# A GRU's state update on VectorE in another order, and the reset product's passes in another order on TensorE

## The chip, the core and the metric

One NeuronCore of a Trainium2 chip runs the whole kernel. The metric is the device time of one execution in microseconds (us); less is better.

## The reference

x is [32, 512, 512] (batch, time, features), the state has 512 features. A conditioned GRU runs over the 512 time steps, and its states are added to x:

```python
vz = video @ C_z + b_z          # vr, vh alike
xz = einsum('btd,de->bte', seq, W_z)   # xr, xh alike
def step(h, xs):
    z = sigmoid(xz_t + h @ U_z + vz)
    r = sigmoid(xr_t + h @ U_r + vr)
    hh = tanh(xh_t + (r * h) @ U + vh)
    h_new = (1 - z) * h + z * hh
```

Everything is float32. Each step needs the state of the one before.

## The kernel before

**Layout.** The 32 x 512 state lies on 128 partitions as four groups of 32 rows, with 128 columns each: partition group j holds features 128 j to 128 j + 127. A 32 x 32 block transpose on VectorE ("turn") makes of it the weights of the next product. Each product is cut into 4 x 4 matmuls of 32 weight columns: q counts the part that is summed over, j the partition group that is written.

**Precision.** x, the gates' weights and the state are split into a high and a low part in float16 (h_hi and h_lo for the state; ur_hi and ur_lo, uz_hi and uz_lo for the weights). Three passes of products, high x high, high x low and low x high, stand for one in float32. The candidate product alone runs in float32.

**One time step,** by the engines' own queues; semaphores alone order them against each other:
- TensorE (`step`, L356 on): the reset product (`reset_product`, L296, its matmul L303, 48 matmuls of 128 columns), the update product (L312, 48), three groups of the x projection of two steps ahead (L276, 12 matmuls of 384 columns), the candidate product (L266, two halves, each after its reset_t), in every fourth step a small total product (L285), and the other nine groups of the projection (36 matmuls). Then the next step's reset product.
- ScalarE: h_hi of half 0 and half 1 from the turned state (L428), the reset gate in two halves (L432), 1 - z and z (L435, L436), the candidate's tanh in two halves (L441), and in three steps of four one operation on x for a later set of steps (L382, L385 or L388).
- VectorE (`go_on` and `begin`): the reset state r * h and its turn for each half (L637, L639), the seeds of the next accumulators with the projections (L518, L523), a turn of x (L514), then for each half `take` (L661: tanh times z), `renew` (L665: plus the kept part, which gives the new state) and `turn` (L669: into h_t), and h_lo for each half (L611: h_t times 2 to the 14th minus h_hi).
- GpSimd: the kept part (1 - z) * h (L223), the low part of x (L210), and x plus the new state (L237), which is sent out by SyncE's queue in blocks of 8 steps.

The halves are halves of the 128 columns, so two of the four q of the next product each: reset_product waits for h_hi of half 0, h_lo of half 0, h_hi of half 1, h_lo of half 1, each ahead of the first pass that uses it. The order on each engine is written out by hand; nothing plans it. The loop on TensorE holds 4 steps, those of the others 64. TensorE's last pass through `step` stands for no time step: the engines raise its semaphores by hand.

Of the kernel before, what the change touches and what calls it, by code (L numbers as in the profile page):

```python
# [5 lines left out]
def conditioned_gru_residual_kernel(nc, x, cond, W_z, U_z, C_z, b_z, W_r, U_r, C_r, b_r, W_h, U_h, C_h, b_h, out):  # L6
# [24 lines left out]
    HALVES = 2  # L31
# [22 lines left out]
    with ctx:  # L54
# [70 lines left out]
        def half(a):  # L125
            return slice(N // HALVES * a, N // HALVES * (a + 1))
# [10 lines left out]
        def part(j):  # L137
            return slice(B * j, B * (j + 1))

        def cols(c):  # L140
            return slice(N * c, N * (c + 1))
# [107 lines left out]
        def _(pe):  # L249
# [44 lines left out]
                total(p_bank[k][:, G * N + c:G * N + c + 1], row_sum, [x_sum[:, of:of + 1]], first).then_inc(x_totaled, 1)  # L294

            def reset_product(out, halves):  # L296
                passes = [(h, a, b) for h in range(HALVES) for a in range(2) for b in range(2 - a)]
                for n, (h, a, b) in enumerate(passes):
                    if b == 0:
                        pe.wait_ge((h_hi_ready, h_lo_ready)[a], halves[h])  # L300
                    for q in range(Q // HALVES * h, Q // HALVES * (h + 1)):
                        for j in range(J):
                            last = nc.tensor.matmul(out[part(j)], (h_hi, h_lo)[a][:, part(q)], ur[b][:, q, cols(j)],  # L303
                                                    start=False, stop=n == len(passes) - 1 and q == Q - 1,
                                                    skip_group_check=True)
                return last
# [49 lines left out]
            def step(m, tt):  # L356
                s = m * SET + tt
                c, k = tt % SET, tt % 2
                now = pe.snap(s + 1)
                halves = [pe.snap(HALVES * s + (a + 1)) for a in range(HALVES)]  # L360
                pe.wait_ge(seeded, now)
                reset_product(cell(k, R), halves).then_inc(r_mm, 1)
                update_product(cell(k, Z)).then_inc(z_mm, 1)
                pe.wait_ge(c_seeded, now)
                pe.wait_ge(x_t_ready, pe.snap(s + 3))
                project(k, (c + 2) % SET, 0, BEFORE_C)
                candidate_product([(reset_t_ready, a) for a in halves])
                if c == TOTAL_STEP:
                    total_x(TOTAL_STEP % 2, 0, 0, pe.snap(m + (tt // SET + 3)), False)
                project(k, (c + 2) % SET, BEFORE_C, GROUPS)  # L370
# [110 lines left out]
        def _(dve):  # L481
# [19 lines left out]
            def least_x(k, m, count):  # L501
                dve.wait_ge(x_link, count(2 * m + 1))
                V.tensor_scalar(x_pow[k][:], x_pow[k][:], LEAST, None, ALU.max).then_inc(x_link, 1)

            def up_x(k, m, count):
                dve.wait_ge(x_link, count(2 * m + 2))
                up_of(x_up[k][:], x_pow[k][:]).then_inc(x_scaled, 1)
# [4 lines left out]
            def turn_x(k, c, sets):  # L512
                dve.wait_ge(x_lo_ready, sets)
                V.transpose(x_t[:, c].rearrange("p n a -> p (n a)").bitcast(i32),  # L514
                            x_parts[k][:, cols(c)].rearrange("p n a -> p (n a)").bitcast(i32)).then_inc(x_t_ready, 1)

            def seed_gates(k, d):
                V.scalar_tensor_tensor(banks[k][:, :, 0:N], p_bank[k][:, 0:GATES * N].rearrange("p (g n) -> p g n", g=GATES),  # L518
                                       x_down[d][:, W_GATES:W_GATES + 1], base[:, 0:GATES], ALU.mult, ALU.add)\
                    .then_inc(seeded, 1)  # L520
# [99 lines left out]
            def go_on(i, tt, last):  # L620
                s = i * STEPS + tt
                m, t = divmod(tt, SET)
                now_m = i * (STEPS // SET) + m
                old, new = state[:, (tt - 1) % SLOTS], state[:, tt % SLOTS]

                def count(v):
                    return v if last else dve.snap(v)

                now = count(s + 1)

                def more(sets):
                    return not (last and m + sets >= STEPS // SET)

                for a in range(HALVES):
                    ready = count(HALVES * s + (a + 1))
                    dve.wait_ge(r_gate, ready)
                    V.tensor_tensor(reset[:, half(a)], gate_r[:, half(a)], old[:, half(a)], ALU.mult).then_inc(reset_ready, 1)  # L637
                    dve.wait_ge(reset_ready, ready)
                    V.transpose(reset_t[:, half(a)], reset[:, half(a)]).then_inc(reset_t_ready, 1)  # L639

                if t == POWER_STEP and more(2):
                    least_x(m % 2, now_m + 2, count)
                if not (last and tt == STEPS - 1):
                    if t == SET - 1:
                        dve.wait_ge(x_down_ready, count(now_m + 2))
                    dve.wait_ge(projected, count(s + 2))
                    seed_gates((tt + 1) % 2, (tt + 1) // SET % 2)
                if t == POWER_STEP and more(2):
                    up_x(m % 2, now_m + 2, count)
                dve.wait_ge(kept_ready, now)  # L650
                if last and tt >= STEPS - TURN_AHEAD:
                    dve.sem_inc(x_t_ready, 1)
                else:
                    ahead_m, c = divmod(tt + TURN_AHEAD, SET)
                    turn_x(ahead_m % 2, c, count(s + (TURN_AHEAD + 1)))

                ready = [count(HALVES * s + (a + 1)) for a in range(HALVES)]

                def take(a):
                    dve.wait_ge(c_gate, ready[a])  # L660
                    V.tensor_tensor(taken[:, half(a)], gate_c[:, half(a)], gate_z[:, half(a)], ALU.mult).then_inc(taken_ready, 1)  # L661

                def renew(a):
                    dve.wait_ge(taken_ready, ready[a])
                    V.tensor_tensor(new[:, half(a)], taken[:, half(a)], kept[:, half(a)], ALU.add).then_inc(h_ready, 1)  # L665

                def turn(a):
                    dve.wait_ge(h_ready, ready[a])
                    V.transpose(h_t[:, half(a)], new[:, half(a)]).then_inc(h_t_ready, 1)  # L669

                take(0)
                renew(0)
                take(1)
                turn(0)
                if last and tt == STEPS - 1:
                    dve.sem_inc(seeded, 1)
                    dve.sem_inc(c_seeded, 1)
                    dve.sem_inc(h_lo_ready, HALVES)
                    dve.sem_inc(reset_t_ready, HALVES)
                renew(1)  # L680
                turn(1)

            begin(0, 0, True)
# [1 line left out]
            with nc.Fori(0, PASSES - 1, engines=[dve.engine], hint_back_edge=True, head_slot={dve.engine: DVE_SLOT}) as i:  # L685
                for tt in range(STEPS):
                    go_on(i, tt, False)
                    begin(i, tt + 1, False)
            for tt in range(STEPS):
                go_on(PASSES - 1, tt, True)  # L690
                if tt < STEPS - 1:
                    begin(PASSES - 1, tt + 1, True)
# [24 lines left out]
```

## Time and profile before

| | us |
|---|---|
| median of 3 runs | 2236.66 (2235.65 to 2237.01) |
| the profiled execution itself | 2234.19 |
| its span, first to last instruction | 2232.4 |
| TensorE matmuls busy | 2179.1 (98%) |
| VectorE busy | 1751.8 (78%) |
| ScalarE busy | 1326.2 (59%) |
| GpSimd busy | 689.1 (31%) |
| granted TensorE clock, mean | 0.999 of full speed |

In the views PE is TensorE's matmuls, PEld its weight loads (which run beside matmuls), DVE VectorE, ACT ScalarE, POOL GpSimd. L303 is line 303 of the kernel. An engine starts an operation before the recorded end of the one ahead of it where nothing holds it, so spacings are read from start to start. The records of matmuls overlap in the same way: four of them, one for each j, run side by side. Rows are rounded to 0.01 us.

### The profile page before, as it was taken

What the parts mean: (1) busy time and instruction counts of PE and PEld (TensorE: products, weight loads), DVE (VectorE), ACT (ScalarE), POOL (GpSimd) and SP (SyncE); (2) the same over time, 40 slices, a digit from 0 to 9 for tenths busy, and PEclk for the clock granted to TensorE, in tenths of its full rate; (3) what the DMA queues carried; (4) which work ended last, traced back from release to release, by engine and by line L of the source; (5) the groups of instructions that cost most, each with busy time, mean ns of one, the idle gap of its engine ahead of it and who ended that gap; (6) DMA issues with size and microseconds to landing.
All of it is one profiled execution on the core that took longest, in us unless ns stands there. A gap on an engine that the chain in (4) does not pass through costs nothing.

```text
span 2232.4 us, 238869 instructions
## 1 busy us (share of the span) xinstructions
PE 2179.1 (98%) x107827; PEld 1805.7 (81%) x107827; DVE 1751.8 (78%) x8225; ACT 1326.2 (59%) x4623; POOL 689.1 (31%) x1546
## 2 busy tenths in 40 slices
PE   1899999999999999999999999999999999999999
PEld 1788888888888888888888888888888888888888
DVE  4678877877777787787777778778777777877876
ACT  3566666666666665666666566566666656656664
POOL 0233333333333333333333333333333333333332
PEclk9999999999999999999999999999999999999999
DMA  9101101101101101111111011011011011011000
GB/s 209 24 20 38 38 19 38 38 19 38 38 19 38 38 19 38 33 25 38 26 32 38 19 38 38 20 38 38 19 38 38 19 38 38 19 39 36 21 19 19
DMA packets 145138, 78.20 MB, mean 35 GB/s; under 512 B 8789, under 2 KB 140373, under 8 KB 144981
## 3 DMA queue, kind: packets, MB, share of 16 engines
q1 hardware_dynamic: 142388, 72.12, 13.4%
q10 hardware_dynamic: 2592, 4.72, 1.0%
q14 instruction: 150, 1.22, 0.2%
q8 instruction: 8, 0.13, 0.0%
HBM read 43.25 MB, written 33.55 MB: 34 GB/s over the span
## 4 chain that ended last, share of the span: by engine, by line
PE 97%; SPq 2%; DMA 1%; issue 0%; DVE 0%; ACT 0%; DVEq 0%
PE p_bank L276 45%; PE c_bank L266 21%; PE banks L303 16%; PE banks L312 15%; SPq L146 1%; DMA c_w<-in_L_cond_C_dram 1%; SPq L164 0%; PE p_bank L285 0%; DVE uz_lo L546 0%; DVE ur_lo L546 0%; SPq L154 0%; SPq L160 0%; PE c_bank L255 0%; DVE reset L637 0%; DVE h_lo L611 0%
## 5 line engine op out<-in xcount | busy, mean ns | idle before, releaser
L276 PE MATMUL p_bank<-w_hi,x_t 128*32 128x384 f16 x16480 | 1188.3, 326 | 0.0
L276 PE MATMUL p_bank<-w_lo,x_t 128*32 128x384 f16 x8240 | 706.9, 326 | 0.0
L276 PEld LDWEIGHTS p_bank<-w_hi,x_t 128*32 128x32 f16 x16480 | 470.2, 97 | 150.2 <-issue 1.5
L266 PEld LDWEIGHTS c_bank<-u,reset_t 128*32 128x32 f32 x32768 | 482.2, 110 | 96.9 <-DVE reset_t L639 95.0
L266 PE MATMUL c_bank<-u,reset_t 128*32 128x64 f32 x32768 | 551.8, 219 | 2.2 <-issue 2.2
L237 POOL TENSOR_TENSOR result<-x_nat,state 128x128 f32<-128x128 f32 x512 | 234.1, 457 | 989.2 <-DVE h_lo L611 987.4
L432 ACT ACTIVATE gate_r<-banks,gates_down 128x64 f32<-128x64 f32 x1024 | 265.6, 310 | 355.0 <-PE banks L303 341.9
L441 ACT ACTIVATE gate_c<-c_bank 128x64 f32<-128x64 f32 x1024 | 228.4, 223 | 288.5 <-PE c_bank L266 288.3
L223 POOL TENSOR_TENSOR kept<-keep,state 128x128 f32<-128x128 f32 x512 | 236.8, 463 | 520.7 <-ACT keep L435 520.7
L637 DVE TENSOR_TENSOR reset<-gate_r,state 128x64 f32<-128x64 f32 x1024 | 208.7, 204 | 205.3 <-ACT gate_r L432 199.1
L428 ACT ACTIVATE h_hi<-h_t 128x64 f16<-128x64 f32 x1024 | 260.8, 255 | 150.2 <-DVE h_t L669 83.2
L303 PE MATMUL banks<-ur_hi,h_hi 128*32 128x128 f16 x8192 | 300.5, 219 | 3.4 <-ACT h_hi L428 3.4
L303 PE MATMUL banks<-ur_hi,h_lo 128*32 128x128 f16 x8192 | 301.4, 221 | 0.0
L303 PE MATMUL banks<-ur_lo,h_hi 128*32 128x128 f16 x8192 | 300.4, 219 | 0.2 <-issue 0.2
L611 DVE SCALAR_TENSOR_TENSOR h_lo<-h_t,h_hi 128x64 f16<-128x64 f32 x1024 | 230.8, 226 | 81.6 <-ACT h_hi L428 80.7
L639 DVE STREAM_TRANSPOSE reset_t<-reset 128x64 f32<-128x64 f32 x1024 | 251.3, 245 | 35.4
L276 PEld LDWEIGHTS p_bank<-w_lo,x_t 128*32 128x32 f16 x8240 | 234.7, 97 | 48.5
L661 DVE TENSOR_TENSOR taken<-gate_c,gate_z 128x64 f32<-128x64 f32 x1024 | 226.5, 221 | 59.6 <-ACT gate_c L441 16.7
L669 DVE STREAM_TRANSPOSE h_t<-state 128x64 f32<-128x64 f32 x1024 | 247.3, 241 | 17.7
L210 POOL TENSOR_TENSOR x_parts<-x_whole,x_parts 128x128 f16<-128x128 f32 (+1 forms) x509 | 237.4, 466 | 28.0 <-ACT x_parts L388 28.0
L518 DVE SCALAR_TENSOR_TENSOR banks<-p_bank,x_down,base 128x256 f32<-128x256 f32 x512 | 236.5, 462 | 3.0 <-issue 3.0
L435 ACT ACTIVATE keep<-banks,gates_minus 128x128 f32<-128x128 f32 x512 | 188.0, 367 | 78.3 <-PE banks L312 72.9
(68 smaller groups left out, 2776.1 us busy)
## 6 DMA issues: line engine op xcount, KB each, us to landing
x_nat<-in_x_dram SPq DMA_DIRECT2D x256, 128.0 KB, 3.1
out_dram<-result SPq DMA_DIRECT2D x252, 128.0 KB, 2.8
w_stage<-in_L_cond_W_r_dram SPq DMA_DIRECT2D x2, 256.0 KB, 5.0
w_stage<-in_L_cond_W_r_dram ACTq DMA_DIRECT2D x2, 256.0 KB, 5.6
w_stage<-in_L_cond_W_z_dram SPq DMA_DIRECT2D x2, 256.0 KB, 9.0
w_stage<-in_L_cond_W_z_dram ACTq DMA_DIRECT2D x2, 256.0 KB, 9.6
w_stage<-in_L_cond_W_dram ACTq DMA_DIRECT2D x2, 256.0 KB, 11.7
u<-in_L_cond_U_z_dram ACTq DMA_DIRECT2D x2, 256.0 KB, 13.5
```

What stands on the lines that cost most here:

```text
L210: return nc.gpsimd.tensor_tensor(x_parts[k][:, part_of, 1], x_whole[k][:, part_of], x_parts[k][:, part_of, 0], ALU.subtract)
L223: nc.gpsimd.tensor_tensor(kept[:], keep[:], state[:, (tt - 1) % SLOTS], ALU.mult).then_inc(kept_ready, 1)
L237: nc.gpsimd.tensor_tensor(result[o][:, t], x_nat[j % BUFS][:, t], state[:, tt % SLOTS], ALU.add)\
L266: last = nc.tensor.matmul(c_bank[part(j), a, 0:N // HALVES], reset_t[:, part(q)], u[:, C, q, half_cols(j, a)], start=False, stop=q == Q - ...
L276: last = nc.tensor.matmul(p_bank[k][part(j), 0:G * N], x_t[:, c, part(q), a], w[b][:, :, q, cols(j)], start=f == 0, stop=f == GROUPS - 1, ...
L303: last = nc.tensor.matmul(out[part(j)], (h_hi, h_lo)[a][:, part(q)], ur[b][:, q, cols(j)], start=False, stop=n == len(passes) - 1 and q == ...
L312: last = nc.tensor.matmul(out[part(j)], (h_hi, h_lo)[a][:, part(q)], uz[b][:, q, cols(j)], start=False, stop=q == Q - 1, skip_group_check= ...
L428: nc.scalar.activation(h_hi[:, half(a)], h_t[:, half(a)], ACT.Copy, scale=2.0 ** POW)\
L432: nc.scalar.activation(gate_r[:, half(a)], banks[k][:, R, half(a)], ACT.Sigmoid, scale=gates_down[:])\
L518: V.scalar_tensor_tensor(banks[k][:, :, 0:N], p_bank[k][:, 0:GATES * N].rearrange("p (g n) -> p g n", g=GATES), x_down[d][:, W_GATES:W_GAT ...
L639: V.transpose(reset_t[:, half(a)], reset[:, half(a)]).then_inc(reset_t_ready, 1)
L669: V.transpose(h_t[:, half(a)], new[:, half(a)]).then_inc(h_t_ready, 1)
```

## The change

In VectorE's part of a step the six operations on the two halves stand in the order take 0, take 1, renew 0, renew 1, turn 0, turn 1; before they stood as take 0, renew 0, take 1, turn 0, renew 1, turn 1. Each keeps its own waits. In the reset product the passes (half h of the state, part a of the state, part b of the weights) were, for each half, (high, high), (high, low), (low, high); now the two passes with the state's high part come for half 0 and for half 1, and then those with the low part for both.

```diff
--- before.py
+++ after.py
@@ -294,7 +294,7 @@
                 total(p_bank[k][:, G * N + c:G * N + c + 1], row_sum, [x_sum[:, of:of + 1]], first).then_inc(x_totaled, 1)
 
             def reset_product(out, halves):
-                passes = [(h, a, b) for h in range(HALVES) for a in range(2) for b in range(2 - a)]
+                passes = [(h, 0, b) for h in range(HALVES) for b in range(2)] + [(h, 1, 0) for h in range(HALVES)]
                 for n, (h, a, b) in enumerate(passes):
                     if b == 0:
                         pe.wait_ge((h_hi_ready, h_lo_ready)[a], halves[h])
@@ -669,15 +669,15 @@
                     V.transpose(h_t[:, half(a)], new[:, half(a)]).then_inc(h_t_ready, 1)
 
                 take(0)
+                take(1)
                 renew(0)
-                take(1)
+                renew(1)
                 turn(0)
                 if last and tt == STEPS - 1:
                     dve.sem_inc(seeded, 1)
                     dve.sem_inc(c_seeded, 1)
                     dve.sem_inc(h_lo_ready, HALVES)
                     dve.sem_inc(reset_t_ready, HALVES)
-                renew(1)
                 turn(1)
 
             begin(0, 0, True)
```

## Rows read from the trace of the kernel before

**Rows 1.** The page: TensorE's busy time; the chain that ended last, by line.
```profile
PE 2179.1 (98%) x107827; PEld 1805.7 (81%) x107827; DVE 1751.8 (78%) x8225; ACT 1326.2 (59%) x4623; POOL 689.1 (31%) x1546
...
PE p_bank L276 45%; PE c_bank L266 21%; PE banks L303 16%; PE banks L312 15%; SPq L146 1%; DMA c_w<-in_L_cond_C_dram 1%; SPq L164 0%; PE p_bank L285 0%; DVE uz_lo L546 0%; DVE ur_lo L546 0%; SPq L154 0%; SPq L160 0%; PE c_bank L255 0%; DVE reset L637 0%; DVE h_lo L611 0%
```

**Rows 2.** The chain by time, 900 to 940 us: start, us, what.
```profile
912.12 0.05 PE p_bank L285 x7
...
913.66 0.67 PE banks L303 x48
...
926.28 0.70 PE banks L303 x48
```

**Rows 3.** Timeline of TensorE's matmuls: start, us, operation, count.
```profile
921.88 0.29 PE L303 MATMUL banks<-ur_hi,h_hi 128*32 128x128 f16 x8
...
923.58 0.34 PE L276 MATMUL p_bank<-w_hi,x_t 128*32 128x384 f16 x4
923.74 1.07 PE L266 MATMUL c_bank<-u,reset_t 128*32 128x64 f32 x64
...
926.10 0.29 PE L303 MATMUL banks<-ur_hi,h_hi 128*32 128x128 f16 x8
...
926.55 0.29 PE L303 MATMUL banks<-ur_lo,h_hi 128*32 128x128 f16 x8
926.68 0.30 PE L303 MATMUL banks<-ur_hi,h_lo 128*32 128x128 f16 x8
926.81 0.29 PE L312 MATMUL banks<-uz_hi,h_hi 128*32 128x128 f16 x8
...
930.38 0.29 PE L303 MATMUL banks<-ur_hi,h_hi 128*32 128x128 f16 x8
```

**Rows 4.** Timeline of TensorE's weight loads; in brackets idle time and its releaser.
```profile
923.72 0.38 PEld L266 LDWEIGHTS c_bank<-u,reset_t 128*32 128x32 f32 x24 [0.19 <-DVE reset_t L639]
...
926.04 0.18 PEld L303 LDWEIGHTS banks<-ur_hi,h_hi 128*32 128x32 f16 x8
...
926.68 0.12 PEld L303 LDWEIGHTS banks<-ur_hi,h_lo 128*32 128x32 f16 x8
...
930.25 0.24 PEld L303 LDWEIGHTS banks<-ur_hi,h_hi 128*32 128x32 f16 x8
```

**Rows 5.** Timeline of ScalarE: the second tanh, then h_hi of both halves.
```profile
924.89 0.22 ACT L441 ACTIVATE gate_c<-c_bank 128x64 f32<-128x64 f32 x1
925.73 0.26 ACT L428 ACTIVATE h_hi<-h_t 128x64 f16<-128x64 f32 x1 [0.62 <-DVE h_t L669]
...
926.12 0.26 ACT L428 ACTIVATE h_hi<-h_t 128x64 f16<-128x64 f32 x1
```

**Rows 6.** Timeline of VectorE in the same step.
```profile
924.92 0.22 DVE L661 TENSOR_TENSOR taken<-gate_c,gate_z 128x64 f32<-128x64 f32 x1
925.18 0.22 DVE L665 TENSOR_TENSOR state<-taken,kept 128x64 f32<-128x64 f32 x1
925.32 0.22 DVE L661 TENSOR_TENSOR taken<-gate_c,gate_z 128x64 f32<-128x64 f32 x1
925.46 0.24 DVE L669 STREAM_TRANSPOSE h_t<-state 128x64 f32<-128x64 f32 x1
925.62 0.18 DVE L665 TENSOR_TENSOR state<-taken,kept 128x64 f32<-128x64 f32 x1
925.84 0.25 DVE L669 STREAM_TRANSPOSE h_t<-state 128x64 f32<-128x64 f32 x1
...
926.40 0.23 DVE L611 SCALAR_TENSOR_TENSOR h_lo<-h_t,h_hi 128x64 f16<-128x64 f32 x1 [0.16 <-ACT h_hi L428]
```

**Rows 7.** Timeline of ScalarE in another step: two h_hi merged.
```profile
1014.61 0.48 ACT L428 ACTIVATE h_hi<-h_t 128x64 f16<-128x64 f32 x2
```

**Rows 8.** Timeline of the matmuls in that step, with a late first load.
```profile
1014.90 0.29 PE L303 MATMUL banks<-ur_hi,h_hi 128*32 128x128 f16 x8
1015.02 0.28 PE L303 MATMUL banks<-ur_lo,h_hi 128*32 128x128 f16 x8
```

## The prediction

> **What bounds the kernel now.** I read the chain of waits first: TensorE holds 97% of it, and its lines are the four kinds of product alone [rows 1]. So only a hole in TensorE's stream can be won or lost. The same chain in a stretch of 17 us, merged by line, shows the holes [rows 2]: the reset product (L303, 48 matmuls) takes 0.67 us at 913.66 and 0.70 us at 926.28, and in that stretch it is 0.70 in three steps of every four, 0.67 in the one that follows the step with the small total product (L285, at 912.12 and again 16.90 us later). Four steps take 16.90 us, and 512 steps are 128 such groups.
>
> Where the 0.035 us goes (the chain rounds it to 0.03; the starts of two reset products, 4.22 us apart at 921.88 and 926.10 [rows 3], against 4.18 in the short step, give 0.04) stands in the matmul rows: the passes start every 0.11 us, but the last goes from 926.55 to 926.68, 0.13, and the update product follows 0.13 later, not 0.11 [rows 3]. The weight load of that pass starts at 926.68 [rows 4], 0.05 after VectorE's second h_lo ends (926.40 + 0.23 = 926.63) [rows 6]. So the last pass waits for h_lo of half 1: about 0.025 of wait, and 0.01 because the stream restarts.
>
> The start of the reset product has no hole. h_hi of half 0 ends at 925.73 + 0.26 = 925.99 [rows 5], its load starts at 926.04 [rows 4], the matmul at 926.10, when the projection before it is through [rows 3]. **The slack of the first half is thus 0.06 us**, and everything below turns on it. In the one step of four that has the total product TensorE comes 0.06 later: load at 930.25 [rows 4], matmul at 930.38 [rows 3], a slack of 0.12 to 0.13.
>
> The candidate product sets nothing new: its load starts at 923.72, after a wait for reset_t [rows 4], its matmul at 923.74, together with the end of the projection pass that precedes it. It is a tie with some 0.02 us to spare, and since the gates' chain starts at the end of the reset product, as TensorE's own work does, it moves with it.
>
> **Part one, VectorE's order.** Now [rows 6]: take 0 at 924.92, sum 0 at 925.18, take 1 at 925.32, turn 0 at 925.46, sum 1 at 925.62, turn 1 at 925.84. No instruction is added or removed; six are sorted anew. An instruction that waits for the result of its predecessor starts 0.26 after it (0.22 long and 0.03 to 0.04 for the semaphore). One that needs nothing new starts 0.14 after it (sum 0 to take 1, take 1 to turn 0), and 0.16 after a turn.
> - Take 1 moves to the front. Its gate is ready when the second tanh ends, 924.89 + 0.22 = 925.11 [rows 5]; with the 0.03 that take 0 needs behind its tanh it starts at 925.14. VectorE stands there from 925.06: with sum 0 behind it in the queue, sum 0 waits too.
> - Sum 0 at 925.28 (it was 925.18), sum 1 at 925.42 (its take ends 925.36, plus 0.04, so it is the spacing that counts), turn 0 at 925.56 (sum 0 ends 925.50 with 0.04 behind it, 925.54, just covered). **Turn 0 is 0.10 later.**
> - Turn 1 at 925.56 + 0.16 = 925.72, not 925.84: **0.12 earlier.**
>
> The trace of before has no two sums in a row. From below, a spacing of 0.10 would follow if each were of the short form, as sum 1 is now (0.18 long, and successors start 0.08 before an end); then turn 0 waits for sum 0 (925.28 + 0.18 + 0.04 = 925.50) and is 0.04 late. From above, 0.16 as behind a turn: 925.14 + 3 x 0.16 = 925.62, 0.16 late. I take 0.14, the row with two plain operations.
> For a queued operation of 64 columns the Trainium skill (Vector Engine (DVE) Microarchitecture Reference, section 5.2, Measured stream behaviour on trn2) states 1.0417 ns a column and about 75 ns fixed, 0.142 us; by it turn 0 would be at 925.57 and the total some 2 to 4 us higher, and the trace's 0.14 and 0.135 agree within the rounding.
>
> ScalarE's h_hi of half 0 follows turn 0: 925.83, ends 926.09, weights at 926.14 by the 0.05 above, matmul at 926.14 to 926.15. It should be at 926.10. That is 0.045 of wait, and again 0.01 for the restart: where a load comes late in the trace, first pass to second is 0.12 and not 0.11 [rows 8]. So the new hole is **0.05 us (0.053 with one digit more in the shift), in three steps of four.** In the fourth the slack of 0.12 becomes 0.12 - 0.10 - 0.035 (TensorE is that much earlier, its old hole gone), just under zero to nothing: I count 0. ScalarE's x work delays nothing: h_hi waited for the turn already.
>
> **Part two, TensorE's order.** Same 48 matmuls, same four waits. The passes need h_hi 0 at the start, h_hi 1 after 0.22 (it was 0.34), h_lo 0 after 0.45, h_lo 1 after 0.56. h_lo 1 then is no longer late: h_hi 1 ends by 926.32 at the worst (below), h_lo 1 by 926.58, ready 926.63, wanted at 926.15 + 0.56 = 926.71. The old hole goes: **-0.035 us, in the three steps that had it.**
> h_hi 1 is the new candidate for being late. Turn 1 ends at 925.72 + 0.25 = 925.97, so it could start at 926.00. ScalarE's own spacing of two h_hi is 0.23 or less (two in 0.48 us [rows 7]), which makes 926.06, an end at 926.31 and weights at 926.37; wanted at 926.15 + 0.22 = 926.37. Covered, by nothing at the upper bound. I count 0; the price if it fails is a rival.
> GpSimd's result add and VectorE's seed of c_bank follow h_lo 1 and start earlier; nobody on TensorE waits for them in that stretch. No DMA is moved.
>
> **Sum.** Three steps x (0.053 - 0.036) = 0.05 us in a group, x 128 = +6.5 us. On the profiled execution's own 2234.19 us (span 2232.4) that is 2240.7; the median shown, 2236.66, is 2.5 above it, and with it I forecast **2243 us**. A hundredth of a microsecond in the shift of turn 0 is 384 x 0.01 = 3.8 us, so this case's own range is 2239 to 2247.
>
> **Rivals.**
> - *The holes cancel.* If the restart costs nothing at the start, or the shift is 0.09, the new hole is 0.03 to 0.045 and the sum -2 to +4 us: 2235 to 2240. For: the two numbers come from rounded rows and are nearly equal. Against: the restart's 0.01 is seen both at a late first pass and at a late last one. Chance 0.27.
> - *Faster, the shift stays inside the slack.* The place is the spacing of sum 0, sum 1 and turn 0. It decides at a shift of turn 0 of 0.06: at the lower bound of 0.04 no hole opens at the start, and the old one is gone. Price -0.035 x 384 = -13 us: 2223. For: sum 1 takes only 0.18 now. Against: that form follows a turn, and the operation queued behind a plain one shows 0.22 and a successor at 0.14. Chance 0.13, with what lies between.
> - *h_hi 1 late.* If two h_hi on ScalarE run 0.26 apart, end to end, half 1 is ready 0.03 too late at the third pass, and it costs 0.03 + 0.01 on top: +0.04 x 384 = +15, 2258. Against it stands the pair in 0.48 us. Chance 0.07.
> - *VectorE does not overlap.* The trace shows take 1 at 925.32 when sum 0 runs to 925.40, which excludes nearly all of it; with ends waited for, turn 0 comes at 925.14 + 3 x 0.22 = 925.80, 0.34 late, a hole of 0.29 for 0.035 saved: 0.255 x 384 = +98 us, 2335. [...] Chance 0.01.
>
> The forecast itself has 0.52. What this kernel's measurement can tell from no change is about 0.2%, 4.5 us: slower by more 0.60 (the forecast, h_hi 1 late, no overlap), within 0.27, faster by more 0.13. The range 2229 to 2254 leaves out most of the faster rival and the two dear ones.
>
> **What would show it.** In the chain after, the reset product is without its late last pass in every step, and a hole of 0.05 stands between the last projection pass and the reset product's first matmul, with h_hi (L428) as releaser, in three steps of four. On VectorE take 1 starts 0.22 after take 0, the sums 0.14 apart, turn 0 0.64 after take 0 (0.54 now). Four steps take 16.95 us. I am wrong if turn 0 comes less than 0.60 after take 0, if the first pass starts without a wait, or if the third pass waits.

## The result and the profile after

The changed kernel takes 2240.18 us (median of 12 runs, 2237.02 to 2241.90), the kernel before 2234.95 us in its 12 runs: ratio 1.0021, 95% interval 1.0014 to 1.0029, so 3 to 6.5 us slower, 4.7 in the middle, and the medians are 5.2 apart. The forecast was 6.5 slower. (It said 2243, 2.8 too high: 1.7 of that is the median of three runs that was shown then, 2236.66, which lay above that of the twelve, and the rest is the change priced too dear.) The interval is clear of no change, and its middle lies on the 0.2% that the chances were stated for. Among the executions behind the times below, one of `e2_tensor_only` ran at a mean granted clock of 0.629 and took 3393.29 us; it is left out of that run's time.

First two more lines of the chain by time of the kernel before, from the same stretch as [rows 2]; columns are start, us, what:

```profile
917.84 0.70 PE banks L303 x48
...
930.56 0.67 PE banks L303 x48
```

From the short reset product at 913.66 [rows 2] to the next at 930.56 is the length of a group of four steps, 16.90 us. The kernel after, same view:

```profile
917.55 0.67 PE banks L303 x48
...
921.73 0.71 PE banks L303 x48
...
925.96 0.71 PE banks L303 x48
...
934.48 0.67 PE banks L303 x48
```

934.48 - 917.55 = 16.93 us. There is still one short product in four, and the other three hold a hole as before. It is another hole. TensorE's matmuls after, to be held against [rows 3]:

```profile
929.85 0.34 PE L276 MATMUL p_bank<-w_hi,x_t 128*32 128x384 f16 x4
930.05 0.29 PE L303 MATMUL banks<-ur_hi,h_hi 128*32 128x128 f16 x8
930.17 0.28 PE L303 MATMUL banks<-ur_lo,h_hi 128*32 128x128 f16 x8
930.28 0.28 PE L303 MATMUL banks<-ur_hi,h_hi 128*32 128x128 f16 x8
930.39 0.28 PE L303 MATMUL banks<-ur_lo,h_hi 128*32 128x128 f16 x8
930.51 0.40 PE L303 MATMUL banks<-ur_hi,h_lo 128*32 128x128 f16 x16
930.73 0.40 PE L312 MATMUL banks<-uz_hi,h_hi 128*32 128x128 f16 x16
```

From the last projection pass to the first of the reset product are 0.20 us, where every projection pass takes 0.16; then 0.12 to the second; and from there on 0.11 (0.12 once, by rounding) to the end: the last pass waits no more. Over the whole trace the medians are 0.199 against 0.163, a wait of 0.036, and 0.010 for the restart: the new hole is 0.046 us. The weight loads name who holds the first pass:

```profile
930.05 0.12 PEld L303 LDWEIGHTS banks<-ur_hi,h_hi 128*32 128x32 f16 x8 [0.24 <-ACT h_hi L428]
```

In the whole trace this wait now occurs 512 times and holds the loads 121.0 us; most of each is time in which a load would only have run ahead of its matmul. VectorE and ScalarE in that step, to be held against [rows 5, 6] (take 0 starts at 928.83):

```profile
929.06 0.22 DVE L661 TENSOR_TENSOR taken<-gate_c,gate_z 128x64 f32<-128x64 f32 x1
...
929.20 0.22 DVE L665 TENSOR_TENSOR state<-taken,kept 128x64 f32<-128x64 f32 x1
...
929.33 0.22 DVE L665 TENSOR_TENSOR state<-taken,kept 128x64 f32<-128x64 f32 x1
929.47 0.24 DVE L669 STREAM_TRANSPOSE h_t<-state 128x64 f32<-128x64 f32 x1
```

```profile
929.74 0.26 ACT L428 ACTIVATE h_hi<-h_t 128x64 f16<-128x64 f32 x1 [0.72 <-DVE h_t L669]
...
929.90 0.24 ACT L428 ACTIVATE h_hi<-h_t 128x64 f16<-128x64 f32 x1
```

Take 1 stands 0.23 behind take 0, the sums 0.14 apart (0.13 in the rounded rows), turn 0 at 0.64 (0.54 before). h_hi of half 0 ends at 930.00, its load starts at 930.05.

**Where the rest is.** 0.034 us in each of 128 groups are 4.4 us (16.934 for 16.900, medians of the whole traces). Seven times, once in 64 steps, a group took 0.16 more. There the second h_hi comes late and the third pass with it:

```profile
874.98 0.28 PE L303 MATMUL banks<-ur_lo,h_hi 128*32 128x128 f16 x8
875.24 0.29 PE L303 MATMUL banks<-ur_hi,h_hi 128*32 128x128 f16 x8
```

ScalarE starts this h_hi at 874.93, 0.38 behind the first (0.16 elsewhere), with its turn long done. The kernel before shows no such group; there h_hi of half 1 starts 0.39 behind the first in every step, so the pause, if ScalarE has it, is covered. It adds 1.1 us. From the fifth reset product to the last the two profiled executions differ by 5.2 us (2147.7 and 2142.6), as the medians do. Their spans differ by 7.0: the other 1.9 us lie ahead of the fifth product, where the first steps run irregularly in every trace.

### The profile page after: what moved, and what is told of

The parts are those of the page before. It is cut to its first block, busy times and chain, and to the rows that moved or that the text cites. A ratio compares the mean times of both kernels' runs of the same rounds, so it can differ in the third digit from the quotient of the medians.

```text
span 2239.4 us, 238869 instructions
## 1 busy us (share of the span) xinstructions
PE 2185.0 (98%) x107827; PEld 1770.1 (79%) x107827; DVE 1698.1 (76%) x8225; ACT 1284.9 (57%) x4623; POOL 689.1 (31%) x1546
## 4 chain that ended last, share of the span: by engine, by line
PE 97%; SPq 2%; DMA 1%; issue 0%; DVE 0%; ACT 0%; DVEq 0%
PE p_bank L276 45%; PE c_bank L266 21%; PE banks L303 16%; PE banks L312 15%; SPq L146 1%; DMA c_w<-in_L_cond_C_dram 1%; SPq L164 0%; PE p_bank L285 0%; DVE uz_lo L546 0%; DVE ur_lo L546 0%; SPq L154 0%; PE c_bank L255 0%; SPq L160 0%; DVE reset L637 0%; DVE h_lo L611 0%
## 5 line engine op out<-in xcount | busy, mean ns | idle before, releaser
L428 ACT ACTIVATE h_hi<-h_t 128x64 f16<-128x64 f32 x1024 | 206.4, 248 | 121.0 <-DVE h_t L669 95.6
L303 PE MATMUL banks<-ur_hi,h_hi 128*32 128x128 f16 x8192 | 266.2, 221 | 3.1 <-ACT h_hi L428 3.1
L611 DVE SCALAR_TENSOR_TENSOR h_lo<-h_t,h_hi 128x64 f16<-128x64 f32 x1024 | 190.7, 226 | 101.9 <-ACT h_hi L428 101.9
L303 PE MATMUL banks<-ur_lo,h_hi 128*32 128x128 f16 x8192 | 262.2, 219 | 0.7 <-issue 0.7
L303 PEld LDWEIGHTS banks<-ur_hi,h_hi 128*32 128x32 f16 x8192 | 145.8, 95 | 122.0 <-ACT h_hi L428 121.0
L312 PE MATMUL banks<-uz_hi,h_lo 128*32 128x128 f16 x8192 | 204.5, 219 | 0.9 <-issue 0.9
```

## The experiments

Two theories stood against each other. Mine: take 1 waits for the second tanh and holds all of VectorE's queue, which opens the hole at the start; TensorE's new order only moves what is wanted when. The rival: the parts are independent, and what VectorE loses is the spacing of its own operations. In what follows a typical group is four steps between two short reset products.

### Each half of the change alone

`e1_vector_only`: VectorE's new order, TensorE's old passes.

```diff
-passes = [(h, 0, b) for h in range(HALVES) for b in range(2)] + [(h, 1, 0) for h in range(HALVES)]
+passes = [(h, a, b) for h in range(HALVES) for a in range(2) for b in range(2 - a)]
```

> Only VectorE's order is the changed one; TensorE keeps the passes of before. My theory (each engine's order alone makes a new wait, and the other half of the change takes most of it away): turn 0 is 0.10 us late as in the changed kernel, so the first pass waits 0.04 to 0.05 us; and the third pass now asks for h_lo of half 0 at 0.23 us after the start, which is ready only at 0.26, so the reset product takes 0.71 to 0.72 us instead of 0.68. That is 0.036 us a step over the changed kernel in three steps of four and 0.024 in the fourth: +17 us over it, some +22 us over the kernel before (2257). Rival (the two halves of the change are independent and add up, and what is lost is lost on VectorE alone): the same time as the changed kernel or a few us less, 2238 to 2240.

Measured: 2257.86 us, ratio 1.0106 (1.0091 to 1.0122).

`e2_tensor_only`: the reverse, that line as in the changed kernel and VectorE as before.

> Only the passes of the reset product are in the changed order; VectorE keeps its order of before. My theory: the first pass starts without a wait, but the third now asks for h_hi of half 1 at 0.22 us, and in the kernel before its load could start only at 0.325: a hole of 0.10 and 0.01 for the restart, and the old hole of 0.036 goes. Net +0.076 us in three steps of four, +0.056 in the fourth: +36 us, 2271. Rival (halves independent): the passes' order saves the old hole, 0.036 x 384 = -14 us, 2221.

Measured: 2272.85 us, ratio 1.0163 (1.0144 to 1.0181), +36 us. The chain of e1 and then the matmuls of e2:

```profile
902.62 0.69 PE banks L303 x48
906.84 0.75 PE banks L303 x48
...
919.69 0.69 PE banks L303 x48
```

```profile
924.80 0.29 PE L303 MATMUL banks<-ur_hi,h_hi 128*32 128x128 f16 x8
924.91 0.29 PE L303 MATMUL banks<-ur_lo,h_hi 128*32 128x128 f16 x8
925.12 0.30 PE L303 MATMUL banks<-ur_hi,h_hi 128*32 128x128 f16 x8
```

In e1 a group takes 17.07 us (902.62 to 919.69): the start is late as in the changed kernel, and the product itself has grown to 0.75, since h_lo of half 0 is late too. In e2 the third pass comes 0.21 behind the second, not 0.11. Both runs came out within 2 us of what was expected (2257 and 2271). One half costs some 24 us, the other 36, and both together 5. The rival falls: the halves are two sides of one order, and each alone makes the other engine wait for the wrong operand.

### Take 1 without its wait for the second tanh

`e3_no_second_tanh`: the changed kernel, where take 1 reads the tanh of half 0.

```diff
-dve.wait_ge(c_gate, ready[a])
-V.tensor_tensor(taken[:, half(a)], gate_c[:, half(a)], gate_z[:, half(a)], ALU.mult)...
+dve.wait_ge(c_gate, ready[0])
+V.tensor_tensor(taken[:, half(a)], gate_c[:, half(0)], gate_z[:, half(a)], ALU.mult)...
 ...
 turn(0)
+dve.wait_ge(c_gate, ready[1])
```

> The changed kernel, but take 1 reads the tanh of half 0, so it need not wait for the second tanh (part of the computation is left out: half 1 of the candidate is not used; a separate wait for the second tanh stands behind turn 0, where it has long been met). My theory (the hole at the start comes from take 1 standing for the second tanh with everything queued behind it): turn 0 starts 0.53 to 0.54 us after take 0 instead of 0.636, the first pass doesn't wait, h_hi of half 1 is in time, so no hole is left: four steps 16.79 us, 2221, some 14 us below the kernel before and 19 below the changed one. Rival (the spacing of the sums and of the turns sets turn 0, not the tanh): turn 0 stays 0.60 or more after take 0 and the time stays at 2238 to 2240.

Measured: 2229.12 us, ratio 0.9970 (0.9958 to 0.9983): half of the gain forecast, though the typical group took 16.79 us exactly. Forty-odd of the others took 0.03 to 0.31 more, at the same steps of every round of 64, and one behind the loop's end 1.6 more, where VectorE stood 1.53 us for nothing that the profile shows. So the added wait instruction was taken out again, save in the last step (`e9_no_second_tanh_clean`):

```diff
 turn(0)
-dve.wait_ge(c_gate, ready[1])
 if last and tt == STEPS - 1:
+    dve.wait_ge(c_gate, ready[1])
```

> As e3_no_second_tanh (take 1 reads the tanh of half 0, so half 1 of the candidate is left out), but without its separate wait instruction in VectorE's stream, save in the very last step. In e3 79 of the groups of four steps took 16.79 us as forecast, and the others 0.05 to 0.33 us more, with VectorE's h_lo or ScalarE's h_hi starting 0.15 to 0.28 us after all they wait for, at the same steps of each round of 64. Theory A (those late starts come with the added instruction, by the place that it gives the others in VectorE's program): they are gone on VectorE here, only ScalarE's one in 64 steps stays, and the time is 2221 to 2225. Theory B (they come with the shorter step itself): the time stays at 2227 to 2231, as in e3.

Measured: 2222.35 us, ratio 0.9942 (0.9928 to 0.9955), 12 to 13 us below the kernel before: theory A. (Like e3 it leaves out half 1 of the candidate and is no kernel to use.) VectorE in a step of e9 (pairs merged), then its chain:

```profile
917.01 0.36 DVE L661 TENSOR_TENSOR taken<-gate_c,gate_z 128x64 f32<-128x64 f32 x2
917.29 0.36 DVE L665 TENSOR_TENSOR state<-taken,kept 128x64 f32<-128x64 f32 x2
917.56 0.37 DVE L669 STREAM_TRANSPOSE h_t<-state 128x64 f32<-128x64 f32 x2
```

```profile
905.77 0.67 PE banks L303 x48
...
914.19 0.67 PE banks L303 x48
918.37 0.67 PE banks L303 x48
922.56 0.67 PE banks L303 x48
```

Turn 0 starts 0.55 behind take 0, the sums at their 0.14, and every reset product here takes 0.67: 905.77 to 922.56 are 16.79 us. All that the changed order needs is the second tanh 0.1 us sooner. The tanh follows the candidate product's second half, so it can't simply be moved forward.

### What binds the kernel before: one move on TensorE

`e7_half_update`: the kernel before, with 0.028 us of the update product ahead of the last reset pass.

```diff
 for n, (h, a, b) in enumerate(passes):
+    if n == len(passes) - 1:
+        # update product, high x high, q = 0, columns 0 to 63 (four matmuls), no longer done later
+        update_product(update_out, ahead=True)
     if b == 0:
         pe.wait_ge((h_hi_ready, h_lo_ready)[a], halves[h])
```

> The kernel before with one thing moved: four matmuls of the update product (high x high, q = 0, the first 64 of their 128 columns, 0.028 us of TensorE's time) stand ahead of the reset product's last pass, which waits for h_lo of half 1. My theory (the loss of the kernel before is this one wait, and the gates' chain behind the reset product ends in a tie with TensorE's own work): the wait of 0.026 is filled, the reset product ends 0.01 earlier than before and TensorE has 0.028 less to do behind it, so 0.027 to 0.036 us go in three steps of four: -10 to -14 us, 2221 to 2225. Rival (the candidate product's wait for reset_t, not TensorE's work, is what really binds): the gates' chain starts at most 0.01 earlier and the time falls by no more than 3 us; in the fourth step, where nothing waits now, it rises by 0.028, so 2232 to 2236.

Measured: 2237.35 us, ratio 1.0005 (0.9996 to 1.0014): no change. My theory falls here and the rival holds, though the time lies 1.4 above the rival's range. The chain to the candidate product, loads and then matmuls:

```profile
922.57 0.13 PEld L266 LDWEIGHTS c_bank<-u,reset_t 128*32 128x32 f32 x4 [0.21 <-DVE reset_t L647]
```

```profile
922.57 1.10 PE L266 MATMUL c_bank<-u,reset_t 128*32 128x64 f32 x64
923.49 0.35 PE L276 MATMUL p_bank<-w_hi,x_t 128*32 128x384 f16 x4
```

In the kernel before the load starts 0.02 to 0.03 ahead of its matmul [rows 3, 4], and the product takes 0.89 to 0.90 to the next. Here TensorE is ready 0.027 sooner, load and matmul start together, and the product takes 0.92. The traces show it in nearly every step: 0.917 in 509 products of e7, where the load has no lead, against 0.893 in the kernel before with a lead of 0.027, and all of the difference lies in the first four matmuls (0.080 for 0.056). What looked like 0.02 us to spare is the lead that this load needs. So the kernel before loses its 0.036 us on a loop of latencies, h_lo of half 1, last pass, gates, reset_t, candidate product, tanh, state, and this reordering on TensorE doesn't win them; others weren't tried.

### Shortening that loop

`e8_gpsimd_take`: take 1 on GpSimd, in the kernel before.

```diff
+pool.wait_ge(c_gate, ...)     # second tanh
+nc.gpsimd.tensor_tensor(taken[:, half(1)], gate_c[:, half(1)], gate_z[:, half(1)], ALU.mult).then_inc(taken_1_ready, 1)
 ...
 take(0)
 renew(0)
-take(1)
 turn(0)
```

> The kernel before with take 1 made by GpSimd, which is idle there (x's low part ends before, the result add comes after), and VectorE's order take 0, renew 0, turn 0, renew 1, turn 1. Nothing is left out. What e7 showed is taken in: the loop is bound by the chain h_lo 1, last pass, gates, reset_t, candidate product, in which nothing can be gained on TensorE alone. My theory: turn 0 need not wait behind take 1 and starts 0.018 earlier (0.26 after sum 0), renew 1 0.16 behind it, so turn 1, h_hi 1, h_lo 1 and the last pass come 0.019 earlier, as long as GpSimd's take is through within 0.42 us of the second tanh: 0.02 in three steps of four, -7 to -8 us, 2228. Rival (GpSimd's operation of two SBUF inputs takes VectorE's sum 0 and turn 0, which run beside it, longer, or its own take and the semaphores are slower than 0.42): no gain or a loss, 2235 to 2250.

Measured: 2254.72 us, ratio 1.0090 (1.0075 to 1.0106): slower than even the rival said. GpSimd's take in a step:

```profile
927.63 0.40 POOL L232 TENSOR_TENSOR taken<-gate_c,gate_z 128x64 f32<-128x64 f32 x1 [0.38 <-ACT gate_c L445]
```

It takes 0.40 us for 64 columns (VectorE 0.22) and starts some 0.07 behind the tanh (VectorE 0.03), 0.47 in all where 0.42 was the limit. VectorE in that step (take 0 starts at 927.37):

```profile
927.88 0.25 DVE L673 STREAM_TRANSPOSE h_t<-state 128x64 f32<-128x64 f32 x1
928.06 0.23 DVE L669 TENSOR_TENSOR state<-taken,kept 128x64 f32<-128x64 f32 x1
928.32 0.24 DVE L673 STREAM_TRANSPOSE h_t<-state 128x64 f32<-128x64 f32 x1
```

Turn 0 is 0.51 behind take 0 and not 0.54, as forecast. But sum 1 is where it was, 0.69 to 0.70 behind take 0, it now takes 0.23 instead of 0.18, and turn 1 comes 0.95 behind take 0, not 0.92. h_hi and h_lo of half 1 are late by that, two passes of the reset product, the fourth and the last, start late instead of one, and a group takes 17.05 us.

`e10_vector_high_part`: h_hi of half 1 on VectorE.

```diff
-for a in range(HALVES):        # ScalarE: h_hi of both halves
+for a in range(1):
 ...
 for a in range(HALVES):        # VectorE: h_lo of both halves
+    if a == 1:
+        dve.wait_ge(h_t_ready, ...)
+        V.tensor_scalar(h_hi[:, half(a)], h_t[:, half(a)], 2.0 ** POW, None, ALU.mult).then_inc(h_hi_ready, 1)
     dve.wait_ge(h_hi_ready, ...)
```

> The kernel before, with h_hi of half 1 made by VectorE (the turned state times 2 to the 14th, to float16) and not by ScalarE; nothing is left out. It shortens the chain that e7 left as the bound: turn 1, h_hi 1, h_lo 1, last pass, gates, reset_t. My theory: in the kernel before h_hi 1 ends 0.291 us after turn 1 and h_lo 1 0.55 after it. VectorE's h_lo 0 starts 0.18 after turn 1 and its spacing is 0.14, so h_hi 1 starts 0.32 after turn 1's start, is 0.18 to 0.22 long (no row shows this operation at this size; the other VectorE operations of 64 columns take that), and h_lo 1 starts 0.03 behind: 0.01 to 0.04 us earlier than now. The last pass waits 0.026 today, so of the 0.036 of hole 0.01 to 0.036 go in three steps of four: -4 to -14 us, 2221 to 2231. Rival (VectorE's queue is too full there: h_lo 0 or the seed of c_bank behind the added operation come late, or the operation takes 0.3 us): no gain or slower, 2235 to 2245.

Measured: 2234.71 us, ratio 0.9997 (0.9988 to 1.0006). Yet the step is shorter. VectorE, and the chain:

```profile
920.29 0.24 DVE L672 STREAM_TRANSPOSE h_t<-state 128x64 f32<-128x64 f32 x1
920.48 0.23 DVE L614 SCALAR_TENSOR_TENSOR h_lo<-h_t,h_hi 128x64 f16<-128x64 f32 x1
920.62 0.19 DVE L612 TENSOR_SCALAR h_hi<-h_t 128x64 f16<-128x64 f32 x1
920.84 0.23 DVE L614 SCALAR_TENSOR_TENSOR h_lo<-h_t,h_hi 128x64 f16<-128x64 f32 x1
```

```profile
912.36 0.67 PE banks L303 x48
916.54 0.67 PE banks L303 x48
920.74 0.68 PE banks L303 x48
...
929.19 0.67 PE banks L303 x48
```

h_hi takes 0.19, h_lo of half 1 starts 0.55 behind turn 1 (0.56 to 0.57 before [rows 6]), and a group takes 16.83 to 16.84 us. 128 x 0.06 is 7.5 us, but most is given back: some 3 us in 21 groups of 16.95 to 17.00, and 3.4 us in two stalls right behind the loop's end, VectorE's and, later, ScalarE's of 2.15:

```profile
1965.30 0.22 DVE L668 TENSOR_TENSOR state<-taken,kept 128x64 f32<-128x64 f32 x1
1966.74 0.23 DVE L664 TENSOR_TENSOR taken<-gate_c,gate_z 128x64 f32<-128x64 f32 x1 [1.22 <-issue]
```

VectorE stands 1.2 us for nothing that the profile shows. So the code's place was changed alone (`e11_high_part_slot`), and then ScalarE's program kept as long as it was, too (`e12_high_part_slot_spare`):

```diff
-PE_SLOT, DVE_SLOT = 0, 8
+PE_SLOT, DVE_SLOT = 0, 200
```

> e10 (h_hi of half 1 by VectorE), with the loop of VectorE placed elsewhere in its instruction memory: slot 200 and not 8 of a block of 256. The usual group of four steps in e10 took 16.84 us and not 16.90, as its forecast had it, worth 7.5 us, but VectorE stood 1.3 us and ScalarE 2.1 us right behind the loop's end, and VectorE 0.14 us twice in each round of 64 steps. The loop is 64 instructions longer on VectorE, so slot 200 gives its end the place in the block that it has in the kernel before. Theory A (these stalls are a matter of where the code lies): VectorE's 1.3 us goes, the 0.14 us may go; ScalarE's 2.1 stays, since its program is as in e10: 2231 to 2234. Theory B (they belong to the step that is shorter now, or to the queue being fuller): as e10, 2234 to 2236.

> As e11, and ScalarE still makes its h_hi of half 1, into a tile that nobody reads, so that its program has the length and the places that it has in the kernel before. Nothing of the computation is left out. Theory A: both stalls behind the loop's end are gone, and the time is 7 to 8 us below the kernel before: 2227 to 2229. Theory B: 2234 to 2236 as e10.

Measured: e11 2228.09 us, ratio 0.9968 (0.9958 to 0.9979); e12 2227.70 us, ratio 0.9969 (0.9958 to 0.9980). In e11 VectorE's stall behind the loop is gone; ScalarE's, which comes a little later, is still there in e11 (the row below) and gone in e12:

```profile
1972.63 0.63 ACT L382 ACTIVATE x_abs<-x_nat 128x512 bf16<-128x512 f32 x1 [2.33 <-issue]
```

That much is as theory A had it. But e11 fell 3 us further than theory A said, and it kept pauses of another kind: 14 of 0.22 us on VectorE, at fixed steps of every round of 64. The traces show where the rest came from. Reset products in the chain, first e10, then e11:

```profile
62.15 1.44 PE banks L303 x48
...
85.95 0.69 PE banks L303 x43
```

```profile
59.74 0.92 PE banks L303 x48
...
82.93 0.66 PE banks L303 x45
```

From the fifth product on e11 is only 1.4 us shorter than e10, about the size of VectorE's stall. The other 3.0 us lie ahead of it. Before the first product TensorE stands idle for 2.8 us in e10 and 1.3 us in e11 and e12. In e10 its granted clock then fell to the lower of its two levels, 1.2 GHz, for most of 62 to 66 us; in e11 it stayed at 2.4 GHz. The windows of 62 to 64 us of e10 and of e11 (the third number from the end is the granted clock):

```profile
62.00:64.00 2.00, 1.85 (x72) 1.85 (x76) 1.03 (x7) 0.46 (x3) 0.45 (x1) 0.56 0.00 0
```

```profile
62.00:64.00 2.00, 2.00 (x88) 1.53 (x80) 1.83 (x10) 1.32 (x5) 0.70 (x2) 1.00 0.03 8
```

The first step takes 5.8 us in e10 and 4.3 in e11. It was no accident of one execution: the mean granted clock is 1.0 in all 15 of e11 and e12, and 0.998 or 0.999 in all 11 of e10; on the chip where e11 ran, the kernel before showed 1.0 once in 14. Since the slot is all that sets e11 apart from e10, the place of VectorE's code shortened the start too; by what path no run shows.

e11 computes all that the reference does, has one operation moved and one constant changed, and **is faster than both kernels: 7 us below the kernel before, some 12 below the changed one.** Of the shorter step alone it keeps less: its span is 5.7 us below that of the kernel before, 2.4 of them ahead of the fifth reset product and 3.3 in all the steps after it.

## Why the prediction was right, point by point

- **TensorE bound, the old hole in the last pass.** Right as to the place, and shown from both sides: e9 has no hole and 16.79 us, which is 16.90 less 3 x 0.036. The reading that TensorE's own work sets the pace there was wrong: e7 gave it less to do and gained nothing.
- **Take 1 waits for the second tanh, turn 0 is 0.10 later, turn 1 0.12 earlier.** Right: 0.64 behind take 0 as forecast; e9 takes away that wait alone and the lag goes.
- **The spacing of queued sums is 0.14.** Right (0.14 and 0.13 in the trace after), so neither bound came true. The estimate of 0.142 from the Trainium skill's two figures (Vector Engine (DVE) Microarchitecture Reference, section 5.2, Measured stream behaviour on trn2) is within the rounding.
- **The new hole, 0.053 us in three steps of four.** The place, the releaser and the restart's 0.01 are right. The size is somewhat large: it measured 0.046, and the group, which I made 16.95, takes 16.93. The term is the wait, the shift of 0.10 less the slack of the first half. The shift was 0.099 in the median, the slack 0.064 where 0.06 or a little less was read from rows of 0.01, so the wait was 0.036 and not 0.043. As the sum takes the difference of two nearly equal holes, 0.017 became 0.011 in each of three steps: 4.4 us and not 6.5. It was luck that the pauses of ScalarE put 1.1 us back on the same side.
- **h_hi of half 1 just in time.** Right in the usual step, and with room: ScalarE's own spacing is 0.16, where I had only 0.23 as an upper bound. Once in 64 steps it was late for a reason that I had not listed, 1.1 us in all.
- **The candidate product "with some 0.02 us to spare".** Wrong, without harm to the sum, since both chains move together: e7 shows nothing to spare.
- **The rivals.** The holes do not cancel, though they come near: 0.046 against the 0.045 that this rival had as its upper end. The shift did not stay inside the slack. VectorE does overlap. (Its price of 98 us left out the fourth step, where a turn 0.34 late would have opened a hole too.)

That each half of the change alone would cost five to eight times as much stands in no line of the prediction; it priced the pair only.

## What to carry to other kernels

Where several engines hand halves of a state around a loop, price the loop through each operand, from its ready time to the product that wants it and back. An order on one engine may be good only with one order on the others, and a part of a change timed alone may say little of the pair. Moving an instruction forward in a queue moves its wait forward for all behind it, so look up when its last operand is ready before counting the spacing. When the usual step gets shorter by what was forecast and the total does not, look for single long steps, and at where the code lies in instruction memory, before giving the idea up. And when the total falls by more than forecast, compare the start apart from the steps: the gain may lie there.

## What the runs showed of the hardware

- A float32 weight load that starts together with its matmul, not 0.03 us ahead, costs the candidate product 0.024 us (0.917 for 0.893, e7 against the kernel before), and a late float16 one 0.010 on the first pass.
- One more instruction in each of the 64 steps of a loop cost VectorE single late starts of 0.15 to 0.28 us at fixed steps and 1.5 us behind the loop's end (e3 against e9, 7 us). After the loop's end e10 lost 1.2 us in the same way, and that the place of the loop's head alone took away (e11). What the engine does in these pauses wasn't shown by any run; that the one in e10 hangs on the code's place was, and for those of e3 it is likely but wasn't tried.
- GpSimd takes 0.40 us for a product of two 128 x 64 float32 tiles, VectorE 0.22.
- Ahead of the first step TensorE stands idle. In the profiled executions of e10 and of the two kernels compared it did so for 2.8 to 3.4 us, and its granted clock was at 1.2 GHz for some 3 us around and after the first product; in those of e11 and e12 it was idle for 1.3 us, and the clock stayed at 2.4 GHz. It stayed there too in those of e1 and e8, after 2.8 and 3.3 us, so the idle time alone doesn't settle it.
